# Expert stage: ScalarE's output copy moved to the front of its step, ahead of the rows' copy and the inner layer's copy

## The reference

```
x = x + time_mix_and_channel_mix(layernorm(x))      # RWKV-style mixing; a scan over the sequence
x = x + experts(layernorm(x))
```

```
gates  = sigmoid(xt @ expert_sel.T)                 # [8192, 32]
val, idx = top_k(gates, 4)                          # the other 28 gates become 0
scores = relu(einsum('nd,edf->nef', xt, keys))      # inner layer: 256 -> 128, per expert
out    = einsum('nef,efv->nv', scores * gate, values)   # 128 -> 256, per expert
```

## Time and profile before

| | us |
|---|---|
| median of 3 runs | 1311.43 |
| lowest and highest | 1310.67 and 1311.70 |
| the profiled execution | 1311.79 |
| its span (first to last instruction) | 1309.9 |
| expert stage: first scatter starts, last one starts | 821.65 and 1199.12 |
| combine stage: to the end of the span | from about 1202 |

### The profile page before, as it was taken

One profiled execution on the slowest core, in us unless ns is written; L12 is line 12 of the kernel. 1 busy time (PEld: TensorE's weight loads), 2 busy tenths in 40 slices (PEclk: granted clock), 3 DMA queues, 4 the chain that ended last, 5 costly groups with the idle time before them and its releaser, 6 DMA issues.

```text
span 1309.9 us, 27758 instructions
## 1 busy us (share of the span) xinstructions
PE 1188.1 (91%) x7372; PEld 1031.5 (79%) x7373; DVE 1034.8 (79%) x2460; ACT 832.6 (64%) x1761; POOL 801.3 (61%) x900
## 2 busy tenths in 40 slices
PE   7799999999999999999999874999999999993765
PEld 6678887888788887878888654999999999992544
DVE  4789889888988898898898677777777777771877
ACT  4468567656856775685676562777777777771443
POOL 2523567666866766686675667677777777774000
PEclk9799999999999999999999985999999999996999
DMA  6001112121221212122121487777666666547999
GB/s 229 1 17 33 57 50 90 65 81 49 81 73 49 89 65 77 53 80 73 49 90 53 146 336 229 226 248 233 204 207 201 209 198 206 175 148 240 411 413 355
DMA packets 119841, 192.80 MB, mean 147 GB/s; under 512 B 17378, under 2 KB 93420, under 8 KB 118384
## 3 DMA queue, kind: packets, MB, share of 16 engines
q1 hardware_dynamic: 82672, 114.03, 27.0%
q0 software_dynamic: 26112, 67.68, 14.2%
q10 hardware_dynamic: 11008, 10.52, 2.3%
HBM read 101.09 MB, written 95.26 MB: 150 GB/s over the span
## 4 chain that ended last, share of the span: by engine, by line
PE 64%; DVE 10%; DMA 9%; ACT 7%; issue 5%; SPq 1%; DVEq 1%; POOL 1%; ACTq 1%; POOLq 0%
PE ps L466 25%; PE ps L1552 11%; DMA ye<-expert_rows 5%; PE ps L1540 3%; PE ps L675 3%; PE ps L669 2%; DMA expert_rows<-y,dest 2%; PE ps L671 2%; PE ps L1533 2%; ACT kr L768 2%; PE ps L613 2%; PE ps L1534 2%; PE ps L1535 2%; PE ps L456 1%; ACT u L798 1%
## 5 line engine op out<-in xcount | busy, mean ns | idle before, releaser
L1663 POOL DMA_INDIRECT expert_rows<-y,dest x288 | 289.1, 1004 | 92.1 <-issue 83.6
L1552 PE MATMUL ps<-xt_hi,keys 128*128 128x128 f32 x1152 | 225.6, 282 | 8.2 <-DVE keys L1621 8.2
L1552 PEld LDWEIGHTS ps<-xt_hi,keys 128*128 128x128 f32 x1152 | 189.7, 195 | 11.9 <-DVE keys L1621 11.6
L1346 POOL DMA_INDIRECT lists<-rows_even,slot x128 | 143.6, 1122 | 42.6 <-issue 38.3
L1346 POOL DMA_INDIRECT lists<-rows_odd,slot x128 | 140.6, 1099 | 42.0 <-issue 39.2
L1552 PE MATMUL ps<-xt_lo,keys 128*128 128x128 f32 x576 | 160.1, 278 | 0.0
L1585 ACT ACTIVATE xt_hi<-ps 128x512 fp32r<-128x512 f32 x144 | 86.3, 599 | 89.2 <-PE ps L1552 86.2
L1632 DVE TENSOR_TENSOR xt_lo<-ps,xt_hi 128x512 fp32r<-128x512 f32 x144 | 99.4, 690 | 40.2 <-ACT xt_hi L1585 39.2
L1621 DVE TENSOR_TENSOR keys<-experts_raw,keys 128x256 fp32r<-128x256 f32 x288 | 109.3, 421 | 16.0 <-issue 14.2
L1582 ACT ACTIVATE keys<-experts_raw 128x256 fp32r x288 | 105.4, 425 | 21.8 <-issue 21.6
L1012 DVE TENSOR_TENSOR k_lo<-ksq,k_hi 128x512 fp32r<-128x512 f32 x128 | 103.2, 822 | 18.7 <-ACT k_hi L777 17.9
(11 more groups left out here) (233 smaller groups left out, 3404.2 us busy)
## 6 DMA issues: line engine op xcount, KB each, us to landing
xr<-lists SPq DMA_DIRECT2D x288, 130.0 KB
ye<-expert_rows SPq DMA_DIRECT2D x32, 1024.0 KB, 21.8
x_sb<-in_x SPq DMA_DIRECT2D x16, 512.0 KB, 3.8
residual<-xp SPq DMA_DIRECT2D x16, 512.0 KB, 4.6
experts_raw<-in_expert_in SPq DMA_DIRECT2D x8, 1024.0 KB, 15.4
resid<-residual SPq DMA_DIRECT2D x4, 2048.0 KB, 12.1
out_dram<-resid ACTq DMA_DIRECT2D x32, 256.0 KB, 11.6
expert_rows<-y,dest POOLq DMA_INDIRECT x288
```

The source lines that it names most:

```text
L1346: pool.indirect_dma_start(lists, bass.IndirectOffsetOnAxis(ap=slot[:, q, n:n + 1], axis=0), rows[q][:, n // TOPK, :], None).then_inc(last_ ...
L1552: mm = pe.matmul(ps[:, H + q % HBANKS, c], keys[:, q, s, half, k * DE:(k + 1) * DE], m[:, q, k, c], start=n == 0, stop=n == 3 * KD - 1)
L1663: pool.indirect_dma_start(expert_rows, bass.IndirectOffsetOnAxis(ap=dest[:, r, s:s + 1], axis=0), y[:, r, s, :], None, bounds_check=OUT_RO ...
```

## The change

The `y` copy of ScalarE's step is moved from the last place behind the wait for `pe_step` to the first. The wait for `sent` moves with it. Nothing is added or taken away, and no other engine's stream changes.

```diff
@@ on_scalar, step(i, r, ring) @@
                 for s, e in enumerate(experts):
                     ins = act.activation(keys[:, q, s, 0, :], raw_keys(e), ACT.Copy)
                 ins.then_inc(keyhi_ready, 1)
+            if lagging(i, Y_LAG):
+                b, q = i - Y_LAG, (r - Y_LAG) % RING
+                act.wait_ge(pe_step, b + Y_LAG + 1)
+                after(act, sent[q], 16 * SUB * (ring if r >= Y_LAG else ring - 1))
+                act.activation(y[:, q].rearrange("p s d -> p (s d)"), ps[:, Y + q % YBANKS, :],
+                               ACT.Copy).then_inc(ycopy_ready, 1)
+            if enters(i):
+                q = r % SLOTS
                 act.wait_ge(pe_step, i + 1)
                 act.activation(xt_hi[:, q].rearrange("p k b -> p (k b)"), ps[:, XT + q, :],
                                ACT.Copy).then_inc(xhi_ready, 1)
@@
                 act.wait_ge(pe_step, b + H_LAG + 1)
                 act.activation(h_hi[:, q, :], ps[:, H + q % HBANKS, 0:BLOCK], ACT.Relu).then_inc(hhi_ready, 1)
-            if lagging(i, Y_LAG):
-                b, q = i - Y_LAG, (r - Y_LAG) % RING
-                act.wait_ge(pe_step, b + Y_LAG + 1)
-                after(act, sent[q], 16 * SUB * (ring if r >= Y_LAG else ring - 1))
-                act.activation(y[:, q].rearrange("p s d -> p (s d)"), ps[:, Y + q % YBANKS, :],
-                               ACT.Copy).then_inc(ycopy_ready, 1)
             if fills and r % (RING // FILLS) == 1:
```

## The result

The changed kernel takes 1316.91 us (median of 12 runs, 1313.86 to 1321.28); the kernel before took 1311.57 us in the same rounds (12 runs, 1308.09 to 1318.3). The ratio is 1.0039, with an interval of 1.0024 to 1.0053: slower by 5.3 us between the medians, where 4.5 was forecast. The profiled execution of the changed kernel lies 1.6 us under its median: 1315.35 us, span 1313.5.

What follows compares the result with a forecast made beforehand. GpSimd's scatters, 2.62 us a block, bound the stage. TensorE 3.8 + 3.1 = 6.9 us late, less 2.4 free, gives 4.5, taking in GpSimd's 2.1: 1316.3 profiled, 1315.9 us for the runs; 8 in 10 from 1310.9 to 1323.

Steps and rivals of the forecast that it cites:

- GpSimd paces, and not TensorE: Expert stage: GpSimd's scatters set the pace at 2.62 us a block; TensorE's step of 2.48 becomes 2.59, still under it.
- Rival B: Expert stage: TensorE becomes the pacemaker, all 137 steps lose 0.20 us; 1326.8 us, chance 0.15.
- The stall a step: TensorE's steps in three stretches of the expert stage: late `h_lo` costs 0.20, 0.11 and 0.11 us a step.
- g - 0.53: VectorE: lateness a step, the time from `xt_lo` to `h_lo` over its new limit; about 0.40, 0.20 and 0.18 us.
- two neighbours share one lateness: TensorE's steps: a stall delays the next signal and gives the next step that much back, so cost is half the lateness.
- wait of 0.43: Kernel before, step with the long table load: TensorE's 0.43 us wait at 1.45 us from `xt_lo` to `h_lo`.
- rival A: Expert stage: TensorE's lateness stays hidden behind GpSimd's pace, only the earlier start counts; 1310.7 us, chance 0.16.
- C: Expert stage: earlier `y` frees GpSimd at every wait, without a new one; up to 3.7 us faster, 1307.7, chance 0.07.
- The three stretches: 3.8, 3.1, 0: TensorE's added lateness in us at 826 to 886, 886 to 964 and 964 to 1179 us; 6.9 in all.
- GpSimd 2.1 late: First stretch: TensorE's 3.8 us less 0.76 of earlier `y` and 0.95 of lead; stays to the last scatter.
- The second gate: 4.5: Stage's end: TensorE 6.9 us late pushes 4 MB of residual into the combine stage's loads; 2.4 lie free, 4.5 us remain.
- Edits costed at nothing: The wait for `sent` moved ahead, row loads and keys' low parts 0.48 us later, zero fills and table loads: no cost.

Runs made afterwards that it cites:

- first_unrolled: Against the kernel before: `y` copy first only in the written-out steps 4 to 31, last in the hardware loop; 1314.16 us, ratio 1.0038.
- mid: Against the kernel before: `y` copy moved to the middle, behind `xt_hi` and ahead of `h_hi`; 1311.57 us, ratio 1.0007.

## Why the prediction was right, and where it wasn't

The forecast of 1315.9 us lies 1.0 under the median. The path that it named is, in outline, the one in the trace: TensorE late through VectorE, and felt at the stage's end through the residual. How it passes there, and several sizes on the way, were otherwise, and in part errors cancelled. Step by step:

- **GpSimd paces, and not TensorE.** Held: in blocks 30 to 138 GpSimd's pace is 2.608 us and was 2.610, though TensorE was busy for 9 us more of the window. Rival B would have put all of TensorE's stall on the end; TensorE ended 7.5 us later, counted from the first scatter, and GpSimd 2.3 at most.
- **`y` 0.76 earlier, the others 0.48 later.** Held: 0.50 and 0.48 between the copies, `xt_lo` 0.50 later.
- **The stall a step.** Forecast 0.20, 0.11 and 0.11; measured 0.18 and 0.118 in the first two stretches. The way there was half wrong. The loads became shorter (medians 0.685 and 0.532 where 0.801 and 0.603 stood). With them the lateness is g - 0.53: 0.29 and 0.13. Of this the steps lost 0.6 and 0.9, not half: "two neighbours share one lateness" isn't borne out in the second stretch. Two errors cancelled, and that is luck. Nor does a row have the "wait of 0.43" that was to confirm the limit on g: in that step TensorE's idle time before line 1533 is 0.20 us.
- **Where it would show.** Wrong: 17 us of waits for `h_lo` in over 80 were forecast, 3.7 in 7 seen. By the prediction's own sign ("those waits stay few") this spoke for A or C, so the sign was badly chosen. A wait is counted where an engine stands idle, and here TensorE's busy time in the window rose by 9.0 us (359.15 against 350.11) for the same kind of steps, and so did the step length: most of the stall is booked as busy. Whoever had read the waits alone would have called it rival A.
- **The three stretches: 3.8, 3.1, 0.** Measured 3.8, 3.5, 0.5; TensorE is 7.5 late counted from the first scatter, 6.8 with that scatter's 0.76 taken off, where 6.9 was forecast. The third stretch went as told: 2.597 where the ring had held it to 2.591, and no lead regained.
- **GpSimd 2.1 late.** Not borne out in size. The 2.1 has the 0.76 taken off; measured in the same way it is 1.5 (379.78 less 377.47 less 0.76), and 0.6 counted from block 0's `xt_hi`. The last scatter starts at 1199.41, not at about 1201. The working was another, too. It starved for 4.7 us more than before (idle beyond the 0.30 is 6.6, was 1.9): 3.1 in the first 60 scatters, 1.5 in one wait at scatter 113, the rest smaller. The prediction had only the first, as 2.1. Against that, 13 fewer scatters were long, which gave back 2.4. The sum took a scatter's mean length as fixed.
- **The second gate: 4.5.** The gate was right, the way through it wrong. Measured from the first scatter, the `ye` load is late by 5.5 - 0.76 = 4.7 us. The words had the 4 MB push into the combine stage's loads. Instead the loads of `ye` aren't slowed (the first takes 5.03, was 4.91); the last scatter's landing is longer, by 3.2 us, and `ye` waits for that. So the two gates lie one behind the other and add up, where the sum took the larger one alone: 1.5 of scatters and 3.2 of landing make the 4.7. That this comes near 4.5 is luck in part. The 2.4 us of free time were about right: the residual went out 5.25 us closer to the last scatter, and the landing grew by 3.2, so that about 2.0 cost nothing (an estimate from these two numbers).
- **Edits costed at nothing.** No wait in the trace contradicts them: TensorE's waits for the keys fell from 6.8 us to 0.4, and one wait for the rows of 1.3 us stands where 0.2 stood.

Still open: why `first_unrolled` loses as much as the full change in its runs, though its TensorE ends on time and its last scatter lands in 2.64 us, and why `mid`, as long from first to last scatter, isn't measurably slower. The 5.3 us of the runs therefore can't be divided. The profiled executions, whose spans differ by 3.6, show 3.2 of landing for certain; a cost of the first gate in the runs isn't shown.

## What to carry to other kernels

When several copies hang on one signal, order them by who waits at their end, and count the wait of the engine behind each: the 0.48 us that `y` put ahead of `xt_hi` went through VectorE into TensorE's steps, 0.18 us in each up to step 30 and 0.12 up to step 60, and the 0.76 that `y` gained didn't make up for it. Look for a stage's second exit before calling slack free: TensorE's last matmul came 13 us ahead of GpSimd's last scatter, but the loads issued at its end had only some 2 to spare. Measure the length of a step, not only the waits: of stalls of 0.1 to 0.2 us a step the waits here showed 3.7 us in 7 rows. And before a difference of 2 us in two traces is called a cost, look whether a kernel that has it is slower: `mid` wasn't, measurably.

## What the runs showed of the hardware

**A scatter is longer when it starts in the first part of one of VectorE's key subtractions.** In the kernel before, each of the 29 long scatters starts inside a pair of them. One of these, and the next scatter, which is short; then VectorE's pair:

```profile
873.71 1.22 POOL L1663 DMA_INDIRECT expert_rows<-y,dest  x1 [0.30 <-issue]
875.24 0.98 POOL L1663 DMA_INDIRECT expert_rows<-y,dest  x1 [0.30 <-issue]
```

```profile
873.32 0.76 DVE L1621 TENSOR_TENSOR keys<-experts_raw,keys 128x256 fp32r<-128x256 f32 x2 [0.71 <-issue]
```

The length falls the later the scatter starts inside a subtraction, and starts anew with the second one of the pair: 1.27 us at 0.01 behind the pair's start, 1.18 at 0.10, 1.10 at 0.18; 1.24 at 0.37, 1.17 at 0.44, 1.09 at 0.52; 0.98 outside. The effect ends before the subtraction does: each takes 0.42 us, and a scatter that starts more than 0.29 us into one isn't lengthened. Of 62 that start inside one, 29 are long. `xt_lo` and `h_lo`, which read PSUM and one tensor in SBUF, never lengthen one. With the subtraction cut to 8 columns no scatter is long (this is `keys_short`; minimum, median and maximum in ns):

```profile
L1664 POOL DMA_INDIRECT expert_rows<-y,dest x288: 982/985/997, 846.1 to 1408.6; - x144
```

The Trainium skill, "SBUF — State Buffer", "SBUF: two separate sides", says that a VectorE operation with two SBUF inputs and a GpSimd operation that reads SBUF hold a shared pair of ports in turn, each for its whole instruction. The rows agree in one direction: the subtractions have two SBUF inputs, and the scatter is late by what is left of one, less about 0.12 us. They don't show the other one: 234 of the 288 subtractions start while a scatter runs, and these take 0.418 us in the median like the rest. Whether a scatter counts as such a GpSimd operation isn't shown either. So a change in VectorE's timing changes the scatters' length with no wait in the trace: 16 long ones in the changed kernel, 29 before, 40 with the load moved. Free of them, GpSimd would need 2 x (0.985 + 0.30), about 2.57 us a block.

**The landing of an indirect scatter** takes 2.1 us with the residual's loads held back behind it (two traces), 2.6 to 2.9 when these 4 MB went out 12.5 to 12.9 us ahead of it (five traces), and 5.83 when they went out 7.6 us ahead (one trace).
